# A decoder layer on one core: ordered first loads, and new instruction lists for all five engines

## The reference

```
x = x + attn(layernorm(x))                 # q, k, v: 256 -> 128; softmax(q k' / sqrt(128)) v; masked by head_mask; w_o: 128 -> 256
x = x + xattn(layernorm(x), ctx, mask)     # xp = relu(W x + b), yp = relu(W ctx + b); softmax(xp yp', masked keys at -inf) ctx
x = x + ffn(layernorm(x))                  # bitlinear(silu(bitlinear(x, w_gate)) * bitlinear(x, w_up), w_down), inner width 1024

bitlinear(a, w): a rounded to 8-bit steps of each row's largest |a|; w rounded to -1, 0 or 1 times its mean |w|
```

## Time and profile before

| | |
|---|---|
| median of 3 unprofiled runs | 427.23 us |
| profiled execution | 429.57 us |
| its span, first to last instruction | 427.8 us |
| PE busy | 381.2 us (89%) |
| ACT busy | 333.5 us (78%) |
| DVE busy | 325.6 us (76%) |
| POOL busy | 291.7 us (68%) |
| mean granted TensorE clock | 0.951 of full |

### The profile page before, as it was taken

One profiled execution on the slowest core, in us unless ns is written; L12 is line 12 of the kernel. 1 busy time (PEld: TensorE's weight loads), 2 busy tenths in 40 slices (PEclk: granted clock), 3 DMA queues, 4 the chain that ended last, 5 costly groups with the idle time before them and its releaser, 6 DMA issues.

```text
span 427.8 us, 7257 instructions
## 1 busy us (share of the span) xinstructions
PE 381.2 (89%) x2131; PEld 293.2 (69%) x2158; DVE 325.6 (76%) x893; ACT 333.5 (78%) x618; POOL 291.7 (68%) x413
## 2 busy tenths in 40 slices
...
DMA packets 50022, 32.18 MB, mean 75 GB/s; under 512 B 43584, under 2 KB 45248, under 8 KB 49600
## 3 DMA queue, kind: packets, MB, share of 16 engines
...
...
## 4 chain that ended last, share of the span: by engine, by line
PE 34%; ACT 16%; DMA 13%; DVE 12%; issue 12%; POOL 11%; SPq 0%; ACTq 0%; POOLq 0%; DVEq 0%
DMA c_half<-c_half 7%; PE d_bank L897 5%; POOL c_work L504 4%; PE b_bank L733 4%; PE b_bank L735 4%; PE b_bank L734 4%; ACT c_half L669 3%; PE g_bank L888 2%; PE u_bank L888 2%; PE a_bank L733 2%; POOL c_work L536 2%; ACT b_xn L574 2%; PE a_bank L735 2%; PE a_bank L734 2%; DVE h_max L1077 2%
## 5 line engine op out<-in xcount | busy, mean ns | idle before, releaser
L504 POOL TENSOR_TENSOR c_work<-c_work 128x512 f32<-128x512 f32 x64 | 82.1, 1287 | 41.1 <-DVE c_work L1065 37.3
L897 PE MATMUL d_bank<-downT,c_half 128*128 128x256 bf16 x256 | 36.8, 291 | 15.9 <-DMA c_half<-c_half 15.2
L536 POOL TENSOR_SCALAR c_work<-c_work,h_q 128x1024 f32<-128x1024 f32 x32 | 36.1, 1128 | 15.1 <-DVE h_q L1084 14.9
L897 PEld LDWEIGHTS d_bank<-downT,c_half 128*128 128x128 bf16 x256 | 24.4, 103 | 28.6 <-DMA c_half<-c_half 23.0
L1065 DVE SCALAR_TENSOR_TENSOR c_work<-c_work,g_bank 128x512 f32<-128x512 f32 x56 | 38.0, 679 | 7.8 <-ACT c_work L659 7.7
L659 ACT ACTIVATE c_work<-g_bank,c_tanh_scale 128x512 f32<-128x512 f32 x56 | 38.8, 692 | 5.1 <-PE g_bank L888 3.7
L662 ACT ACTIVATE c_work<-u_bank 128x512 f32<-128x512 f32 x56 | 33.7, 602 | 11.3 <-POOL c_work L504 7.3
L1077 DVE TENSOR_REDUCE h_max<-c_work 128x1 f32<-128x1024 f32 x32 | 38.8, 1212 | 4.8 <-POOL c_work L504 4.7
L669 ACT ACTIVATE c_half<-c_work 128x1024 bf16<-128x1024 f32 x32 | 34.0, 1063 | 9.5 <-POOL c_work L536 9.5
L733 PE MATMUL b_bank<-ctx_hi,b_pT_hi 128*128 128x256 f32 x128 | 38.2, 298 | 0.3 <-DVE b_nmax L1053 0.3
L734 PE MATMUL b_bank<-ctx_lo,b_pT_hi 128*128 128x256 f32 x128 | 36.1, 282 | 0.0
...
## 6 DMA issues: line engine op xcount, KB each, us to landing
...
c_work<-in_w_gate SPq DMA_DIRECT2D x1, 1024.0 KB, 8.6
c_work<-in_w_up SPq DMA_DIRECT2D x1, 1024.0 KB, 10.5
c_half<-in_w_down SPq DMA_DIRECT2D x1, 1024.0 KB, 12.5
...
```

Of the source, the lines that this page charges most:

```text
L504: pool.tensor_tensor(h[:, t % 2, half * HALF:(half + 1) * HALF], th[:, j % 2, :], up[:, j % 2, :], ALU.mult).then_inc(hs, 1)
L536: pool.tensor_scalar(h[:, t % 2, :], h[:, t % 2, :], h_q[:, t:t + 1], ROUND, ALU.mult, ALU.add).then_inc(h_rounds, 1)
L897: mm = pe.matmul(d_bank[:, 0:D], h_T[:, t % 2, f, :], downT[:, f, :], start=f == 0, stop=f == FC - 1)
```

## The change

The twelve loads become steps of stream W in `SP_ORDER` (`W.x0`, `W.qkv`, ...; x of batch 1 and `ctxT` of batch 0 become ordinary entries of stream S). All five tables are replaced; each step keeps its code, and each table has the same steps as before, but for those loads. One wait is new: `quantise_h` on POOL, before it writes `h_out` of a tile, waits until the same tile's DN result of the batch before has been added.

The core of the diff; of the tables the first lines of two stand for all:

```diff
@@ DVE_ORDER @@
-    A.bn0/0 A.bn1/0 A.ag0/0 A.ag1/0 W.lo/0 A.sh0/0 A.sh1/0 A.bn0/1 W.split/0 A.XT0/0 A.XT1/0 A.ag0/1 A.bn1/1
-    W.sum0/0 W.sum1/0 A.sh0/1 W.sum2/0 A.Q/0 A.K/0 A.VT/0 A.ag1/1 W.sum3/0 A.S0/0 A.S1/0 A.S2/0 A.S3/0 A.sh1/1
-    W.sum4/0 W.sum5/0 A.inv/0 A.P0/0 A.P1/0 A.P2/0 A.P3/0 A.bn0/2 A.bn1/2 A.ag0/2 A.ag1/2 A.bn0/3 A.bn1/3
+    A.bn0/0 A.ag0/0 A.bn1/0 A.sh0/0 A.ag1/0 W.split/0 A.sh1/0 W.lo/0 W.sum0/0 A.XT0/0 A.XT1/0 W.sum1/0 W.sum2/0
+    W.sum3/0 A.Q/0 W.sum4/0 A.K/0 A.VT/0 A.bn0/1 A.S0/0 A.S1/0 A.ag0/1 A.S2/0 W.sum5/0 A.S3/0 A.sh0/1 A.bn1/1
+    A.P0/0 A.P1/0 A.inv/0 A.P2/0 A.P3/0 A.ag1/1 A.bn0/2 A.bn1/2 A.ag0/2 A.sh1/1 A.bn0/3 A.ag1/2 A.bn1/3 A.sh0/2
...
@@ SP_ORDER @@
-    S.ctx/0 S.mask/0 S.x/2 S.ctxT/1 S.mask/1 S.x/3 S.mask/2 S.ctx/1 S.ctxT/2 S.ctxT/3 S.mask/3 S.xqT0/0 S.ctxT/4
+    W.x0/0 W.qkv/0 S.ctxT/0 W.x1/0 W.W/0 W.o/0 W.bias/0 W.hm/0 W.down/0 S.ctx/0 W.gate/0 S.mask/0 W.up/0 S.x/1
+    S.ctxT/1 S.mask/1 S.ctx/1 S.x/2 S.mask/2 S.x/3 S.ctxT/2 S.ctxT/3 S.mask/3 S.ctx/2 S.xqT0/0 S.ctxT/4 S.xqT1/0
...
@@ sync @@
-            for half in range(2):
-                sp.dma_start(x_all[:, 0, 2 * half:2 * half + 2, :], x[:, 0, 2 * half:2 * half + 2, :]).then_inc(x0_loaded[half], 16)
-            sp.dma_start(W_raw, W.rearrange("p c d -> p (c d)")).then_inc(W_loaded, 16)
-            load_ctxT(0)
...
+            def load_first(name):
+                if name[0] == "x":
+                    half = int(name[1])
+                    sp.dma_start(x_all[:, 0, 2 * half:2 * half + 2, :], x[:, 0, 2 * half:2 * half + 2, :]).then_inc(x0_loaded[half], 16)
+                elif name == "W":
+                    sp.dma_start(W_raw, W.rearrange("p c d -> p (c d)")).then_inc(W_loaded, 16)
...
             def step(stream, name, n):
-                if name == "ctx":
+                if stream == "W":
+                    load_first(name)
+                elif name == "ctx":
                     load_ctx(n)
@@ quantise_h @@
                 pool.tensor_scalar(h[:, t % 2, :], h[:, t % 2, :], h_q[:, t:t + 1], ROUND, ALU.mult, ALU.add).then_inc(h_rounds, 1)
+                if n > 0:
+                    pool.wait_ge(c_added, T * (n - 1) + t + 1)
                 pool.tensor_scalar(h_out[:, t:t + 1], h_s[:, t:t + 1], c_out_scale[:, t:t + 1], 1.0, ALU.mult, ALU.mult).then_inc(h_outs, 1)
```

More of the change, by code:

```diff
@@ L43 @@
     A.XT0/0 A.XT1/0 E.YP0/0 A.V/0 A.Q/0 A.K/0 A.VT/0 E.YP1/0 A.S0/0 A.S1/0 A.S2/0 A.S3/0 A.P0/0 A.P1/0 A.P2/0
[L44 to L57, removed]
@@ L180 @@
[L180 to L187 removed]
+    A.P3/0 E.YP0/1 A.H/0 E.YP1/1 A.Y0/0 A.Y1/0 W.total/0 A.XT0/1 A.XT1/1 E.YP0/2 A.V/1 A.Q/1 A.K/1 B.XT0/0
```

274 lines of the change are left out of this document (145 added, 129 removed).

## The result

The changed kernel takes 407.1 us (median of 4 runs, 406.2 to 407.76) against 427.3 us for the kernel before in the same session: ratio 0.9518, 95% interval 0.9486 to 0.955. The forecast was 422.0 us with a range of 416.4 to 427.2. The direction was right, the size was not: 20.2 us instead of 5.2. The profiled execution took 406.57 us, its span is 404.7 us (427.8 before), its mean clock 0.968.

The account below looks back on a forecast made before the run. The prediction took input waits to bound the front, PE's own work the middle and stream C's chain the end. Front 5.2 us, middle 0 and end 0 off 427.23 us gave 422.0 us, range 416.4 to 427.2.

Parts of the forecast that it names:

- What bounds the kernel now: Whole kernel: waiting front, middle of PE's own work (at most 10.1 us to save), end with stream C's chain alone.
- The loads: Front's loads: from bytes issued ahead, w_o lands at about 10.3 us, w_gate at 17.3, the mask at about 17.8.
- The front, step by step: Start up to H: V later at 19.9 us, mask stall gone, scores at 28.0, H at 37.0; gain 5.2 us.
- The middle: PE's stretch between front and end: work unchanged, waits short and spread; 0 taken, between -2.6 and +5 us.
- The end: Last part: stream B ends up to 4.9 us earlier, no gain by itself; 0 taken, between -4.9 and +4.9 us.
- POOL's new wait: POOL before writing `h_out`: bites at DN1 of batch 4 alone; costed at nothing, about 1.6 us without cover.
- (b): Rival, middle and end: DN waits (2.6 us) and a third of POOL's idle time (3) go too; 416.4 us, chance 0.18.
- (c): Rival, front: V waits for w_gate and the clock stays at 1.2 GHz; slower, 429.6 us, chance 0.12.
- (d): Rival: front gains, middle loses the same as later stream C starves PE; within 0.2%, 427 us, chance 0.08.

Follow-up runs that it names:

- h_front2: Second run of h_front, for its trace: changed kernel's order up to batch 0's first attention addition, the order before for the rest; 0.9856 of the time before.
- the e kernels: Four variants of the changed kernel with entries of the front reordered, in three of them also loads; 0.9528, 0.965, 0.9871 and 0.9756 of the time before.
- h_front: Hybrid: changed kernel's order and loads up to batch 0's first attention addition (39.2 us), the order before for the rest; 0.9838 of the time before.
- h_body: Hybrid: order and loads before up to batch 0's first attention addition (48.9 us), the changed kernel's order for the rest; 0.9708 of the time before.
- e_sums: Changed kernel with two DVE sums moved later: w_gate's first behind x's low halves, one over w_down behind V's; 0.9528 of the time before.
- l280: Hybrid: the order before up to 280 us, the changed kernel's order for the rest; 0.9882 of the time before.

## Why the prediction was wrong, by its steps

- **"What bounds the kernel now"**: right that the pieces are front, middle and end, and that what the front gains moves the middle as a whole. h_front2 shows it, and so do the constant distances of the e kernels.
- **"The loads"**: w_o was put at 10.3 and came by 9.03, w_gate at 17.3 and came by 15.59. The count of bytes is right to 1 or 2 us only. The distance between the two is 6.6 us (7.0 taken). The prediction says that it goes by 418 GB/s, but it took the landing of w_up before; 2.62 MB in 7.0 us are 374 GB/s, and at 418 w_gate would have been put at 16.6.
- **"The front, step by step"**: mechanism right, size near. ACT's stall on the mask is gone and PE's 3.67 us with it; V, at 18.15, waits for the sum over w_gate as told, but for 0.78 us. Nine matmuls at 1.2 GHz were a choice. In the profiled execution V, Q and K all ran at the high level (4.4 us); in h_front2 they took 6.5 us (6.1 taken), and its scores start at 26.96, nearer to the forecast's 28.0. 5.2 us became 6.2 and 6.9 by the medians of h_front2 and h_front, and 6.9 by the means at A.Y0/0; the 9.4 of the two traces is that plus luck. The low clock from 24 to 34 us, which the prediction read as a loss of the kernel before, is there in two of the six traces with that front, in part in one, and hardly in three.
- **"The middle"**: this is the step that failed. It says "Between -2.6 and +5 I take 0, for PE's waits are all short and spread". The 2.6 us were the waits for one releaser. The window had said 10.1 us of idle PE time, and between the same places 8.6 us of it are gone (9.8 idle against 1.3). That waits are short and spread is no ground for holding them: a full new order removes them one by one, and only the window's idle time is a bound. I had the bound in the first paragraph and then didn't use it. That paragraph's "at most 10.1 us" was itself too low, since work can leave the middle too.
- **"The end"**: 0 was taken since "this isn't a gain by itself". PE's 3.2 us more of work behind B's last step (23.2 against 20.0 us) did come, in an end that is 39.2 us instead of 39.9, at the cost of idle time there. But it came out of the middle, which is as much shorter. The forecast counted the move's cost in the end and its gain nowhere. With the middle's 8.6 this makes 11.8; h_body measured 12.5 by its ratio. So nearly all of the 14.9 us by which the forecast was off lie here and in the middle. The prediction had said that an error above 5 us would mean that the middle isn't PE's own work alone, and that is what it was.
- **POOL's new wait**: taken at nothing; no run shows a price, and up to 3 us aren't excluded.
- **The rivals**: (b), 416.4, lay nearest. It had the right places, the DN waits and POOL's idle time, and 5.6 us for what measured 12.5. (c) didn't happen, though e_sums and h_front2 show that its clock is real. (d) didn't: h_front2 shows that even the old middle keeps what the front gives.

What stays open: which of the many moves of the body bring its 12.5 us. l280 puts 5 of them behind 280 us. Single families of entries moved by themselves brought no gain in any list; that the gain isn't a sum of such moves is likely by this, and not shown.
